# The third and fourth quarter of the attention probabilities turned by a DMA transpose instead of TensorE

## The reference

```python
q = fq_sym(q * scale, axis=-1); k = fq_sym(k, axis=-1); v = fq_sym(v, axis=2)   # round to 255 levels
attn = einsum('bhqd,bhkd->bhqk', q, k)
attn = softmax(attn, axis=-1)
attn = fq_unsigned(attn, axis=-1)      # each row in whole numbers 0..255 of its maximum
out = einsum('bhqk,bhkd->bhqd', attn, v)
```

## Time and profile before

| | us |
|---|---|
| median of 3 runs (444.6 to 445.2) | 444.75 |
| the profiled execution's own time | 444.33 |
| its span in the trace, first to last instruction | 442.2 |
| score stage in the trace, first to last maxima | 212.16 to 384.43 |
| granted TensorE clock over the span | 1.000 |

### The profile page before, as it was taken

How to read it: one execution, slowest core, us unless ns; L and a number is a source line. 1 busy time by engine, 2 the same in 40 slices (tenths; PEclk the granted TensorE clock), 3 DMA queues, 4 the chain that set the end, 5 groups by cost and what they waited for, 6 DMA issues and landing times.

```text
span 442.2 us, 9394 instructions
## 1 busy us (share of the span) xinstructions
PE 407.3 (92%) x3854; PEld 304.5 (69%) x3854; DVE 363.4 (82%) x593; ACT 314.1 (71%) x402; POOL 105.4 (24%) x177
## 2 busy tenths in 40 slices
PE   8989899999999999999689999999999999888897
PEld 4878778865555554577357777777777777765586
DVE  2836662889999999896999999999999999855343
ACT  3255934788888775554799999999999999931110
POOL 3100402044444444101253333321111111100000
PEclk9999999999999999999999999999999999999999
DMA  7899913311111000459354445444555553000000
GB/s 273 303 426 304 192 64 104 160 42 23 29 25 27 27 0 0 178 227 450 157 192 191 191 191 193 191 192 191 209 199 191 194 192 167 3 1 0 2 0 24
DMA packets 13204, 63.32 MB, mean 143 GB/s; under 512 B 5962, under 2 KB 8682, under 8 KB 9706
## 3 DMA queue, kind: packets, MB, share of 16 engines
q1 hardware_dynamic: 12586, 59.19, 36.4%
q0 software_dynamic: 576, 3.54, 2.2%
HBM read 61.58 MB, written 1.15 MB: 142 GB/s over the span
## 4 chain that ended last, share of the span: by engine, by line
PE 43%; DVE 40%; issue 10%; ACT 4%; DMA 1%; SPq 1%; DVEq 0%; ACTq 0%
DVE arena L1360 18%; DVE w L1360 8%; PE ps L1643 6%; PE ps L1753 5%; PE ps L1652 5%; DVE arena L1370 4%; PE ps L2016 4%; PE ps L1536 2%; PE ps L1600 2%; PE ps L1692 2%; PE ps L2027 2%; DMA arena<-in_segg 1%; PE ps L1560 1%; PE ps L1892 1%; PE ps L1465 1%
## 5 line engine op out<-in xcount | busy, mean ns | idle before, releaser
L1360 DVE CUSTOM_DVE_ANT_0 arena<-ps,arena 128x1024 f32<-128x1024 f32 x88 | 108.5, 1285 | 0.0
L1869 PE MATMUL ps<-arena 128*128 128x512 bf16 x256 | 75.9, 377 | 15.1 <-DVE arena L1360 14.9
L976 ACT ACTIVATE arena<-arena 128x4096 uint8<-128x4096 f32 x21 | 78.0, 3714 | 4.1 <-POOL arena L672 3.4
L1892 PEld LDWEIGHTS ps<-cst,arena 128*128 128x128 f32 x512 | 62.9, 140 | 24.2 <-ACT arena L976 0.9
L1892 PE MATMUL ps<-cst,arena 128*128 128x128 f32 x512 | 76.8, 273 | 0.8 <-ACT arena L990 0.8
L1905 PE MATMUL ps<-vrow,arena 128*128 128x16 f16 x1024 | 59.7, 169 | 0.7 <-DVE arena L1370 0.6
L1905 PEld LDWEIGHTS ps<-vrow,arena 128*128 128x128 f16 x1024 | 53.2, 97 | 2.6 <-DVE arena L1370 1.3
L1360 DVE CUSTOM_DVE_ANT_0 w<-ps,arena 128x1024 f32<-128x1024 f32 x40 | 49.8, 1285 | 0.0
L990 ACT ACTIVATE arena<-ps 128x512 f32<-128x512 f32 x91 | 47.2, 586 | 2.1 <-PE ps L1892 2.1
L1904 PE MATMUL ps<-vrow,arena 128*128 128x16 f16 x728 | 47.6, 170 | 0.2 <-ACT arena L990 0.2
L1904 PEld LDWEIGHTS ps<-vrow,arena 128*128 128x128 f16 x728 | 44.9, 96 | 0.3 <-ACT arena L990 0.3
(11 more groups left out here) (271 smaller groups left out, 693.8 us busy)
## 6 DMA issues: line engine op xcount, KB each, us to landing
arena<-ks_scr SPq DMA_DIRECT2D x16, 2048.0 KB, 8.2
arena<-in_w SPq DMA_DIRECT2D x1, 4488.0 KB, 23.1
arena<-in_columns SPq DMA_DIRECT2D x4, 1024.0 KB, 7.8
arena<-in_w0b SPq DMA_DIRECT2D x1, 2560.0 KB, 16.4
w<-in_w SPq DMA_DIRECT2D x1, 2286.0 KB, 11.5
arena<-in_w SPq DMA_DIRECT2D x1, 2048.0 KB, 8.0
arena<-in_fill SPq DMA_DIRECT2D x1, 2048.0 KB, 9.5
arena<-bc_scr SPq DMA_DIRECT2D x14, 128.0 KB, 3.1
```

Source lines behind the costliest of these rows:

```text
L976: act.activation(out8[:, :, 0], s_sb[u % 3], ACT.Exp, bias=nb[:, u % 3:u % 3 + 1], accum_out=zall[:, u:u + 1]).then_inc(p_ready, 1)
L1360: dve.tensor_tensor_reduce(s_sb[slot][:, keys], ps[:, 2 * (c % 2):2 * (c % 2) + 2, :].rearrange("p a n -> p (a n)"), ksb[h % 2][:, keys], ...
L1869: mm = pe.matmul(bank(2 * (c % 2) + m, 0, 512), qz[h // 8][:, h % 8, b * L:(b + 1) * L], kT[:, h // 8, k:k + 512], start=True, stop=True)
L1892: mm = pe.transpose(bank(4 + n % 3, k * P, P), words[:, w:w + P], ident)
```

## The change

A new constant `TURNED` = 2. TensorE turns only quarters 0 and 1 of units 0 to 30. Quarters 2 and 3 are turned by one DMA transpose a unit on the SP queue, from `p8` straight to a new SBUF buffer `ptd[u % 2]` (512 KB, 128 x 2048 16-bit values). Unit 31 is turned by TensorE as before, with 16-bit transposes for quarters 2 and 3.

- `on_vector`: VectorE evicts quarter 0 only of every fourth unit (and of units 30 and 31), quarter 1 of unit 30, quarters 0 to 2 of unit 31. ScalarE evicts the rest: quarters 0 and 1 in three units of four, quarter 1 in the fourth.
- The turned quarters of the DMA carry the 1024, so their eight matmuls each have their -1024 matmul as well.
- SP: `turned_by_dma(u)` waits for `probabilities(u)` and for `weighted(u - 2, 3)`, then issues the transpose. `head_scales` is cut in two DMAs of 1024 KB a head, issued between the transposes, each as soon as its half of `ksb` has been read for the last time.
- ScalarE: `probabilities(u)` also waits for the transpose of unit u - 2 to land. TensorE: `weighted(u, 2)` and `weighted(u, 3)` wait for the transpose of u.
- `value_rows` of quarters 2 and 3 take their keys without the stride of two, to match the order that the DMA gives.
- Three semaphores of earlier stores are merged into one (`stored`), with the same waits.

The diff, cut to its core:

```diff
+TURNED = 2
 def on_vector(u, c):
-    return c == 0 or u == LAST - 1 or (u == LAST and c < 3)
+    return (u % 4 == 0 or u >= LAST - 1) if c == 0 else ((u == LAST - 1 and c < TURNED) or (u == LAST and c < 3))
...
-        ptr = take([4, 1024], F16)
+        ptr = take([TURNED, 1024], F16)
+        ptd = [take([16, P], F16), w1[:, KEYS:KEYS + 1024].bitcast(F16).rearrange("k (t q) -> k t q", q=P)]
...
-            head_scales(0)
-            head_scales(1)
+            def head_scales(h, k):
+                keys = slice(k * KEYS // 2, (k + 1) * KEYS // 2)
+                sp.dma_start(ksb[h % 2][:, keys], ks_scr[h:h + 1, keys].partition_broadcast(P).rearrange("p o k -> p (o k)"))\
                   .then_inc(ld_ks[h % 2], 16)
...
-            for h in range(2, H):
-                sp.wait_ge(s_read, 8 * (h - 2) + 8)
-                head_scales(h)
+            def turned_by_dma(u):
+                sp.wait_ge(p_ready, u + 1)
+                if u >= 2:
+                    sp.wait_ge(ptr_used, 4 * (u - 2) + 4)
+                sp.dma_start_transpose(ptd[u % 2], p8[:, u % 2, 2 * TURNED * 1024:2 * KEYS].bitcast(F16)).then_inc(ld_pt[u % 2], 16)
+            sp.wait_ge(s_read, 6)
+            head_scales(2, 0)
+            for u in range(LAST):
+                turned_by_dma(u)
+                h = (u + 5 - (u + 1) % 2) // 2
+                k = (u + 1) % 2
+                if h < H:
+                    sp.wait_ge(s_read, 4 * (2 * h - 3) + 2 * k + 2)
+                    head_scales(h, k)
...
                 if u >= 2:
-                    act.wait_ge(t_ps, 4 * (u - 2) + 4)
+                    act.wait_ge(t_ps, TURNED * (u - 1))
+                    act.wait_ge(ld_pt[u % 2], 16 * (u // 2))
...
-                for c in range(1, 4):
+                for c in range(4 if unit == LAST else TURNED):
                     if not on_vector(unit, c):
                         columns16(unit, c)
...
-                    if c == 1:
+                    if c == 1 and on_vector(unit, 0):
                         columns16(unit, 0)
...
+                if c < TURNED or u == LAST:
+                    evicted(TURNED * u + c)
+                else:
+                    pe.wait_ge(ld_pt[u % 2], 16 * (u // 2 + 1))
...
-                        mm = pe.matmul(bank(7, u * HW, HW), ptr[:, c, k * 2 * P + par:(k + 1) * 2 * P:2],
+                        turned = (ptr[:, c, k * 2 * P + par:(k + 1) * 2 * P:2] if c < TURNED
+                                  else ptd[u % 2][:, t - 8 * TURNED, :])
+                        mm = pe.matmul(bank(7, u * HW, HW), turned,
...
-                    turned_over(unit, c)
+                    if c < TURNED:
+                        turned_over(unit, c)
```

More of the change, by code:

```diff
@@ L69, with unit_chunk @@
 LAST = UNITS - 1
+TURNED = 2
 def on_vector(u, c):
-    return c == 0 or u == LAST - 1 or (u == LAST and c < 3)
+    return (u % 4 == 0 or u >= LAST - 1) if c == 0 else ((u == LAST - 1 and c < TURNED) or (u == LAST and c < 3))
+def unit_chunk(n):
+    return (min(n // TURNED, LAST), n - TURNED * min(n // TURNED, LAST))
 def on_vector_until(n):
-    return sum(on_vector(k // 4, k % 4) for k in range(n + 1))
+    return sum(on_vector(*unit_chunk(k)) for k in range(n + 1))
 class Chain:
@@ L353, in perceiver_kernel @@
         kc_sb = sem("kc_sb")
-        st_kv = sem("st_kv")
+        stored = sem("stored")
         ld_kvg = sem("ld_kvg")
@@ L389, in perceiver_kernel @@
         dt_sb = sem("dt_sb")
-        st_bc = sem("st_bc")
         ld_w3a = sem("ld_w3a")
@@ L409, in perceiver_kernel @@
         ld_p8 = sem("ld_p8")
+        ld_pt = [sem(f"ld_pt{k}") for k in range(2)]
         neg_set = sem("neg_set")
@@ L521, in key_rows @@
                 sp.wait_ge(kc_sb, 3 * b + 3)
-                sp.dma_start(kv_scr[b * L:(b + 1) * L, :, :], krow[:, b, :, 0:KVC]).then_inc(st_kv, 16)
+                sp.dma_start(kv_scr[b * L:(b + 1) * L, :, :], krow[:, b, :, 0:KVC]).then_inc(stored, 16)
             key_rows(0)
@@ L526, in _ @@
             sp.dma_start(w1[:, kv_at:W1], w1_d[:, kv_at:W1]).then_inc(ld_wkv, 16)
-            sp.wait_ge(st_kv, 32)
+            sp.wait_ge(stored, 32)
             for j in range(WIN):
@@ L544, in _ @@
             sp.wait_ge(dt_sb, 2)
-            sp.dma_start(bc_scr.rearrange("s a t -> a s t"), bcT[0:2 * DS, :]).then_inc(st_bc, 16)
-            sp.wait_ge(st_bc, 16)
+            sp.dma_start(bc_scr.rearrange("s a t -> a s t"), bcT[0:2 * DS, :]).then_inc(stored, 16)
+            sp.wait_ge(stored, 32 + 16)
             for n in range(2, DS):
@@ L554, in _ @@
                 sp.dma_start(ks_scr.rearrange("h (j a p) -> a h j p", a=2 * CT, p=P)[a], ksT[a * H:(a + 1) * H, :, :])\
[L555 to L559, removed]
+                  .then_inc(stored, 16)
+            sp.wait_ge(stored, 32 + 16 + 16 * 2 * CT)
+            def head_scales(h, k):
+                keys = slice(k * KEYS // 2, (k + 1) * KEYS // 2)
+                sp.dma_start(ksb[h % 2][:, keys], ks_scr[h:h + 1, keys].partition_broadcast(P).rearrange("p o k -> p (o k)"))\
                   .then_inc(ld_ks[h % 2], 16)
-            head_scales(0)
-            head_scales(1)
+            for k in range(2):
+                head_scales(0, k)
+            for k in range(2):
+                head_scales(1, k)
             sp.wait_ge(vq_ready, 4)
             sp.dma_start(w3b, w3_d[:, w3a:W3]).then_inc(ld_w3b, 16)
-            for h in range(2, H):
-                sp.wait_ge(s_read, 8 * (h - 2) + 8)
-                head_scales(h)
+            def turned_by_dma(u):
[12 more added lines that the diff above has]
+                    head_scales(h, k)
             for b in range(B):
@@ L984, in columns16 @@
             def columns16(u, c):
-                n = 4 * u + c
+                n = TURNED * u + c
                 act.wait_ge(t_ps, n + 1)
                 if u:
-                    act.wait_ge(ptr_used, n - 3)
-                act.activation(ptr[:, c, :].bitcast(F32), bank(4 + n % 3, 0, 512), ACT.Copy).then_inc(ptr_sb[1], 1)
+                    act.wait_ge(ptr_used, 4 * u + c - 3)
+                columns = ptr[:, c, :] if c < TURNED else ptd[u % 2][:, 8 * (c - TURNED):8 * (c - TURNED) + 8, :].rearrange("k t q -> k (t q)")
+                act.activation(columns.bitcast(F32), bank(4 + n % 3, 0, 512), ACT.Copy).then_inc(ptr_sb[1], 1)
             act.wait_ge(ld_p8, 16)
@@ L1356, in maxima @@
                     if b == 0:
-                        dve.wait_ge(ld_ks[h % 2], 16 * (h // 2) + 16)
+                        dve.wait_ge(ld_ks[h % 2], 32 * (h // 2) + 32)
                 dve.wait_ge(s_ps, 4 * u + c + 1)
@@ L1364, in columns16 @@
             def columns16(u, c):
-                n = 4 * u + c
+                n = TURNED * u + c
                 dve.wait_ge(t_ps, n + 1)
                 if u:
-                    dve.wait_ge(ptr_used, n - 3)
-                dve.tensor_scalar(ptr[:, c, :], bank(4 + n % 3, 0, 512).bitcast(F16), -1024.0, None, ALU.add).then_inc(ptr_sb[0], 1)
+                    dve.wait_ge(ptr_used, 4 * u + c - 3)
+                columns = ptr[:, c, :] if c < TURNED else ptd[u % 2][:, 8 * (c - TURNED):8 * (c - TURNED) + 8, :].rearrange("k t q -> k (t q)")
+                dve.tensor_scalar(columns, bank(4 + n % 3, 0, 512).bitcast(F16), -1024.0, None, ALU.add).then_inc(ptr_sb[0], 1)
             for unit in range(2):
@@ L1378, in _ @@
                         maxima(unit + 2, c)
-                    if c == 1:
+                    if c == 1 and on_vector(unit, 0):
                         columns16(unit, 0)
                 if unit == LAST - 1:
-                    for c in range(1, 4):
+                    for c in range(1, TURNED):
                         columns16(unit, c)
@@ L1835, in value_rows @@
                     k = (8 * q + t - t % 2) * P + t % 2
-                    mm = pe.transpose(bank(6 - n % 2, 0, 512).bitcast(BF16)[:, t * P:(t + 1) * P], vqb[:, m, k:k + 2 * P - 1:2],
-                                      identb[:, :])
+                    rows = vqb[:, m, k:k + 2 * P - 1:2] if q < TURNED else vqb[:, m, (8 * q + t) * P:(8 * q + t + 1) * P]
+                    mm = pe.transpose(bank(6 - n % 2, 0, 512).bitcast(BF16)[:, t * P:(t + 1) * P], rows, identb[:, :])
                 mm.then_inc(vr_tr, 1)
@@ L1873, in evicted @@
             def evicted(n):
-                if on_vector(n // 4, n % 4):
+                if on_vector(*unit_chunk(n)):
                     pe.wait_ge(ptr_sb[0], on_vector_until(n))
@@ L1885, in turned_over @@
                     pe.wait_ge(p_ready, UNITS + c - 1)
-                n = 4 * u + c
+                n = TURNED * u + c
                 if n >= 3:
                     evicted(n - 3)
[L1889 to L1892, removed]
+                if c < TURNED:
+                    words = p8[:, u % 2].bitcast(F32)
+                    for k in range(4):
+                        w = (4 * c + k) * P
+                        mm = pe.transpose(bank(4 + n % 3, k * P, P), words[:, w:w + P], ident)
```

(20 more changed lines are left out.)

1 line of the change is left out of this document (removed).

## The result

| | before | after |
|---|---|---|
| median of 4 runs, us | 444.77 | 459.76 |
| profiled execution, us | 444.33 | 459.21 |
| its span, us | 442.2 | 457.4 |
| mean granted TensorE clock | 1.000 | 0.963 |
| VectorE busy in the span, us | 363.4 | 351.6 |

The changed kernel takes 1.030 of the time before (95% interval 1.027 to 1.033), some 14.5 to 15 us more. The forecast was 431.9 us, with 456 as the upper end.

The account below looks back on a forecast made before the run. VectorE was taken to bound the score stage. Evictions -13.4 us and tail and run-in +0.5 gave -12.9: profiled 444.33 becomes 431.4, median 431.9 us. The range was 430.5 to 456, the forecast's own 430.5 to 434.

Parts of the forecast that it names:

- VectorE's pace: Score stage: VectorE, busy for all of its 172.27 us, sets the pace; 22 evictions fewer at 0.61 us save 13.4 us.
- The mean unit: Score stage: VectorE's unit becomes 4.81 us in three cases of four, 5.42 in the fourth, 4.96 on average.
- ScalarE's following exponential: ScalarE in the score stage: with two copies a unit takes 4.75 us, under VectorE's 4.81, so no cost.
- A transpose alone: DMA: a 512 KB transpose lands in 4.1 us, by ordinary long-row transfers; the far end was 15.5 us.
- ScalarE's new wait: In `probabilities(u + 2)`, which overwrites the slot transpose u reads: 5.83 us to land, margin 1.7 us at 4.1.
- the part on the queue: SP queue: scale loads 2.7 us a unit plus transpose 1.35 make 4.05 of 4.96 us; SP's order costs nothing.
- B: Rival, 8%: on the shared queue, a transpose after a half load lands in 6.8 us; unit 5.3 us, 441 us total.
- A: Rival, 26%: slow transpose, felt in ScalarE's new wait, slower from 7.05 us landing; 469 us at 8.7.
- Its loop: ScalarE's wait for the transpose of two units ago: two units last 3.79 us plus the landing time.
- A's mild part: Slow transpose landing in up to 7.8 us: unit 5.8 us, 456 us total; 7 of that rival's 26%.

Follow-up runs that it names:

- e1: The changed kernel with only the transposes of units 0 and 1 issued, later units using stale data: 434.5 us, 0.976 of the kernel before.
- e3: The changed kernel without the key scale loads of heads 2 to 15, transposes kept: 435.0 us, 0.976 of the kernel before.
- e8: e3 with a second 512 KB transpose a unit, which nothing but the next of its kind waits for: 455.3 us, 1.020 of the kernel before.
- e5: The changed kernel with transposes reading a constant tile (the keys) and ScalarE's wait for them removed: 459.6 us, 1.032 of the kernel before.
- e2: The changed kernel with ordinary copies of the same bytes in place of the transposes, same waits: 438.5 us, 0.981 of the kernel before.
- one-quarter version: The changed kernel with TensorE turning three quarters and the DMA one (256 KB a unit), evictions reshared: 436.7 us, 0.979 of the kernel before.

## Why the prediction was wrong

**Right.** VectorE's pace and the worth of its evictions: 13.4 us were forecast for 22 of them, and with the transfers out of the way (e1) the profiled execution is 12.6 us under the profiled one before, the median 10.7. The mean unit, 4.96 forecast, 4.98 in e1 and e3. ScalarE's following exponential after 4.75 us, 4.66 where it did not wait. TensorE did not bind. A transpose alone lands nearly as estimated, 4.1 us against 4.3 to 5.2 in e3. Where a late transfer would be felt, ScalarE's new wait, is where it was felt first.

**The step that failed** is in the part on the queue: "the transpose at that rate adds 1.35 us. The sum is 4.05 of 4.96 us." The row that it came from is that of the scale loads. The landing time of one transfer and the time it takes of the engines are two prices, and I had bounded only the first from both sides; the second I took from ordinary loads without a bound. Measured, it is 2.8 us by itself (e8), some 3.0 beside the scale loads (5.71 - 2.7), and 3.3 by its packets' time (e3). With 2.8 the same sum reads 5.5 us, above 4.96 and even above the 5.42 of the kernel before, and forecasts a kernel slower by some 2 us in the stage. Of the 0.75 us by which the unit missed the forecast (4.96 to 5.71) this price explains 0.54; the other 0.2 is the remainder of e8. The same part said that SP's order costs nothing and gave an issue no time; SP was held for 88 of 100 us. How much of the 2.8 to 3.0 us is issuing and how much the engines' work stays open.

**The rivals.** B had the right place, the shared queue, but took over the wrong engine time and so came out as a small gain, 441 us. A had the sign and the symptom, a landing past 7.05 us, and 26%; its mechanism, a transpose that lands late by itself, was not what happened, as e3 shows. Its loop would give P = (3.79 + 7.3) / 2 = 5.55 us, near the 5.71 measured, and could have passed for the cause, had e5 not kept the time with the loop gone. The Trainium skill's figure of 350 to 400 GB/s (Advanced Engine Details and Errata, section X-Bar Transpose (TRN2)) was not reached in any run here: 524 KB in 2.79 us is 188 GB/s (e8). By the packets' time it is 159 GB/s (e3, 10.66 MB in 66.9% of 100 us), against 391 GB/s for the scale loads by the same measure (9.67 MB in 49.5% of 50 us). Its other figure (VectorE: DVE Perf Modes, section The three transpose paths), 1309 ns for one 128 x 128 block, does not add up over the blocks of one transfer: sixteen in one DMA land in 4.3 to 5.2 us (e3), not in 20.9.

**Left out.** The tail and the clock. The 4.5 us after the exponential of unit 30 had no term; TensorE's granted clock is 0.90 over this rest, 1.00 before. The rest is as long in e3 (65.3 us, clock 0.92) and e2 (66.0 us, 0.87), where the stage is fast, and 62.2 us in e1 (0.95) against 62.0 before. So most of the 4.5 us does not need the price of the transposes beside the loads and goes with the lower clock; how much the clock makes was not isolated. The upper end of 456 us took A's mild part only up to L = 7.8; 459.8 lay 4 us past it.

## What to carry to other kernels

For a new transfer next to a standing one, make two sums: its landing time against the slack of whoever waits, and its time on the sixteen engines, added to what else runs there in the same period. Bound the second for the kind of transfer, not by the bytes. If the engines come out full, removing a wait only moves it; transfer less, as the one-quarter version does, and spend the rest of the budget on the engine that had slack. Look at the issuing engine as well: if its timeline has no pause, its own period is the period of the loop.

## What was not expected of the hardware

A DMA transpose of 512 KB takes about twice the engine time of an ordinary transfer of its size (2.8 us from e8, 3.3 by packets' time in e3, against 1.35 at the rate of the scale loads), though alone it lands about as early as a plain copy does beside the scale loads (4.3 to 5.2 us against 5.1 to 5.6). Issuing it holds the SP queue for 1.75 us in the idle tail and up to 5.8 us beside the scale loads, while a plain copy of the same bytes holds it for 0.47 us beside them (e2):

```profile
292.95 0.47 SPq L583 DMA_DIRECT2D arena<-arena  x1
293.46 0.59 SPq L568 DMA_DIRECT2D arena<-ks_scr  x1
```
